# A transformer block on one core: the set-up's loads, modulation, key weights, gates, clears and expert rests in another order

## What is computed

```python
mod = (silu(c) @ wmod).reshape(8, 6, 1, -1)
sa, ca, ga, sb, cb, gb = ...                      # six vectors of 256 for each sequence
ga, gb = sign(g) * max(abs(g), 0.25)
h = layernorm(x) * (1 + ca) + sa
c_q = h @ w_dq.T;  q_c, q_r = c_q @ w_uq.T, c_q @ w_qr.T     # 16 heads of 16 and of 64
c_kv = h @ w_dkv.T;  k_c, v = c_kv @ w_uk.T, c_kv @ w_uv.T
k_r = h @ w_kr.T
q_r, k_r = rope(q_r, k_r)
attn = softmax(causal(([q_c, q_r] @ [k_c, k_r].T) * scale)) @ v
x = x + ga * (attn @ w_out.T)
h = layernorm(x) * (1 + cb) + sb
x = x + gb * experts(h)          # 8 experts of 96, weighted by group from a softmax's top 8 of 32
```

## Time and profile before

| | us |
|---|---|
| median of three runs | 1074.29 |
| lowest and highest run | 1073.05, 1078.35 |
| the profiled execution, its own time | 1071.56 |
| the profiled execution, its span | 1069.9 |

### The profile page before, as it was taken

One profiled execution on the slowest core, in us unless ns is written; L12 is line 12 of the kernel. 1 busy time (PEld: TensorE's weight loads), 2 busy tenths in 40 slices (PEclk: granted clock), 3 DMA queues, 4 the chain that ended last, 5 costly groups with the idle time before them and its releaser, 6 DMA issues.

```text
span 1069.9 us, 23954 instructions
## 1 busy us (share of the span) xinstructions
PE 983.8 (92%) x9847; PEld 724.0 (68%) x9847; DVE 744.9 (70%) x1459; ACT 393.9 (37%) x716; POOL 488.4 (46%) x414
## 2 busy tenths in 40 slices
PE   5899989999899999999899998998989998999887
PEld 4556667766686667866678666865768666776566
DVE  7588586784868768686686848777586876856454
ACT  4234433443333443344332442244323343424322
POOL 1535534645346551654426553374525554266212
PEclk9999989999899998998899998998989999999999
DMA  6421010300102010210102101030011101011000
GB/s 195 119 90 61 2 59 1 100 31 14 48 17 84 31 55 7 69 41 22 60 2 70 61 2 59 2 99 32 16 45 41 59 32 60 1 51 60 2 1 21
DMA packets 37599, 48.73 MB, mean 46 GB/s; under 512 B 9386, under 2 KB 23210, under 8 KB 37490
## 3 DMA queue, kind: packets, MB, share of 16 engines
q1 hardware_dynamic: 37490, 47.20, 13.2%
HBM read 17.80 MB, written 4.21 MB: 21 GB/s over the span
## 4 chain that ended last, share of the span: by engine, by line
PE 73%; DVE 9%; issue 5%; ACT 4%; SPq 3%; POOL 3%; DMA 2%; POOLq 0%; DVEq 0%; ACTq 0%
PE ring L1206 17%; PE ring L1053 11%; PE ring L1054 10%; PE ring L1055 10%; PE av L1222 6%; PE ring L1178 6%; SPq L537 3%; ACT pt L734 3%; DVE prod L916 2%; DVE mcol L940 2%; PE ring L1283 2%; PE ring L1284 2%; PE ring L1285 2%; PE ring L1190 2%; DMA cont<-h_lo 2%
## 5 line engine op out<-in xcount | busy, mean ns | idle before, releaser
L734 ACT ACTIVATE pt<-ring 128x384 f32<-128x384 f32 (+1 forms) x384 | 171.0, 532 | 259.7 <-PE ring L1206 224.6
L940 DVE TENSOR_REDUCE mcol<-ring 128x1 f32<-128x128 f32 (+3 forms) x512 | 212.0, 483 | 44.3 <-PE ring L1183 44.1
L1206 PE MATMUL ring<-rows 32*128 32x512 f32 (+3 forms) x3072 | 189.8, 335 | 9.7 <-issue 2.5
L916 DVE TENSOR_TENSOR prod<-ring,table 128x1024 f32<-128x1024 f32 x128 | 154.2, 1218 | 49.9 <-PE ring L1055 47.9
L1206 PEld LDWEIGHTS ring<-rows 32*128 32x128 f32 x3072 | 137.3, 187 | 67.3 <-issue 35.6
L619 POOL TENSOR_SCALAR_AFFINE_SELECT pt<-pt 128x512 f32<-128x512 f32 x128 | 80.0, 638 | 204.1 <-ACT pt L734 204.0
L592 POOL TENSOR_TENSOR rows<-prod,rows 128x1024 fp32r<-128x1024 f32 x64 | 154.6, 2431 | 7.8 <-ACT rows L713 7.4
L585 POOL TENSOR_TENSOR prod<-prod 128x512 f32<-128x512 f32 x64 | 82.2, 1284 | 158.1 <-DVE prod L916 158.0
L1178 PE MATMUL ring<-rows 32*128 32x512 f32 (+3 forms) x1024 | 78.9, 364 | 20.3 <-ACT pt L734 8.8
L1222 PE MATMUL av<-pt,vals 128*17 128x512 f32 (+3 forms) x1024 | 89.9, 453 | 2.8 <-POOL pt L619 2.8
L1178 PEld LDWEIGHTS ring<-rows 32*128 32x128 f32 x1024 | 44.3, 193 | 63.7 <-issue 37.8
(11 more groups left out here) (188 smaller groups left out, 1858.0 us busy)
## 6 DMA issues: line engine op xcount, KB each, us to landing
cont<-h_hi SPq DMA_DIRECT2D x96, 128.0 KB, 2.0
cont<-h_lo SPq DMA_DIRECT2D x96, 128.0 KB, 2.0
xn<-x_dram SPq DMA_DIRECT2D x8, 512.0 KB, 4.6
xr<-x_dram SPq DMA_DIRECT2D x8, 512.0 KB, 4.2
out_dram<-xr SPq DMA_DIRECT2D x8, 512.0 KB, 3.2
gate_bc<-gates_scratch SPq DMA_DIRECT2D x8, 256.0 KB, 4.8
pt<-wmod_dram SPq DMA_DIRECT2D x1, 1536.0 KB, 6.4
pt<-gup_t_dram SPq DMA_DIRECT2D x16, 96.0 KB, 2.5
```

Of the source, the lines that this page charges most:

```text
L734: sc.activation(pt[:, PT_AT[n] + h * w:PT_AT[n] + (h + 1) * w], ps[:, 0:w], ACT.Exp, scale=SCALE).then_inc(exp_ready.sem, 1)
L916: ve.tensor_tensor(prod[:, s % PROD, :, :], ps[:, :].unsqueeze(1).broadcast_to([P, 2, S]), table[:, :, :], ALU.mult).then_inc(rotated.sem, 1)
L940: last = ve.reduce_max(mcol[:, q, h * HR + ONE_ROW:h * HR + ONE_ROW + 1], ps[:, at:at + (q + 1) * P], AX_X)
L1206: last = pe.matmul(places[h][:, at:at + w], k[head, j * P:(j + 1) * P], q[head, q0:q0 + w], start=p == 0 and at == 0, stop=done, skip_grou ...
```

## The change

The set-up's order and the split of its work are rebuilt. Nothing else is changed but the place of `spread`, which moves from the end of the set-up into the first body.

- Loads: x and the first two of the modulation's six parts go ahead; the other four parts go behind the rotary tables. The register loads of the experts' numbers stand ahead of SP's wait for the modulation, no longer behind it.
- `mod` becomes two steps of 8 products: `mod.0` at the start, `mod.1` and `gates` behind `rope.0011`.
- `split_k` becomes two steps: columns 0 to 255 (subtraction on DVE) and columns 256 to 1,023 (subtraction on GpSimd). ACT rounds both behind the first modulation, no longer ahead of it.
- DVE's clears go to GpSimd (whole tiles), the constants behind the first two rotations.
- The subtraction for the experts' gate and up weights goes from DVE to GpSimd.

```diff
 def setup_steps():
-    out = [("silu",), ("stats1", 0), ("pow1", 0), ("norm1", 0), ("mod",), ("split_d",), ("split_k",), ("turn1", 0, 0), ("turn1", 0, 1),
-           ("gates",), ("modulate1", 0, 0), ("low1", 0, 0), ("modulate1", 0, 1), ("low1", 0, 1), ("fuse", 0), ("split_uv",)]
+    out = [("silu",), ("stats1", 0), ("pow1", 0), ("norm1", 0), ("split_d",), ("mod", 0), ("turn1", 0, 0), ("turn1", 0, 1),
+           ("modulate1", 0, 0), ("low1", 0, 0), ("modulate1", 0, 1), ("low1", 0, 1), ("split_k", 0), ("fuse", 0), ("split_k", 1)]
...
+latent.0 latent_hi.0 latent_lo.0 rope.0000 rotate.0000 rope.0001 rotate.0001 combine.000 consts. split_uv. fuse.1
+kcon.00 kcon_hi.00 kcon_lo.00 move_k.00 rope.0010 rotate.0010 rope.0011 rotate.0011 combine.001 hi.000 mod.1 gates.
...
-            sp.dma_start(wmod_st, wmod.rearrange("(c p) n -> p c n", p=P)).then_inc(ld_mod, 16)
             sp.dma_start(xn[:, :, :], x_rows(0, 0)).then_inc(x_loaded.sem, 16)
+            sp.dma_start(wmod_st[:, :, 0:2 * E], wmod_src[:, :, 0:2 * E]).then_inc(ld_mod, 16)
...
+            sp.dma_start(wmod_st[:, :, 2 * E:6 * E], wmod_src[:, :, 2 * E:6 * E]).then_inc(ld_mod_rest, 16)
...
             sp.wait_ge(ld_idx, 16)
-            sp.wait_ge(mod_read, 1)
+            chosen_at = [sp.value_load(idx_sb[0:1, g:g + 1], min_val=0, max_val=NX - 1) for g in range(G)]
+            sp.wait_ge(mod_read, 2)
             sp.wait_ge(gates_read, 1)
-            chosen_at = [sp.value_load(idx_sb[0:1, g:g + 1], min_val=0, max_val=NX - 1) for g in range(G)]
...
+            pool.wait_ge(mask_made, 1)
+            pool.memset(wuk_l0[:, :].bitcast(F32), 0.0)
+            pool.memset(wuv_l0[:, :].bitcast(F32), 0.0)
+            for part_of in (1, 3):
+                pool.memset(cont[:, :, part_of, :].bitcast(F32), 0.0)
+            pool.memset(spread[:, :].bitcast(F32), 0.0)
+            pool.memset(wT[:, :].bitcast(F32), 0.0).then_inc(pool_setup, 1)
...
+                    if kind == "split_k" and step[1] == 1:
+                        pool.wait_ge(keys_hi_ready, 3)
+                        for k in range(EC):
+                            last = pool.tensor_tensor(keys_to(wk_lo, k, 1), keys_from(k, 1), keys_to(wk_hi, k, 1).bitcast(F32),
+                                                      ALU.subtract)
+                        last.then_inc(keys_lo_rest, 1)
+                    elif kind == "split_ffn":
+                        k = step[1]
+                        pool.wait_ge(ffn_hi_ready, k + 1)
+                        pool.tensor_tensor(gu_lo[:, k, :], gu_st[:, k, :], gu_hi[:, k, :].bitcast(F32), ALU.subtract)\
+                            .then_inc(ffn_split, 1)
...
                         for k in range(EC):
-                            sc.activation(wk_hi[:, k, :].rearrange("p (b h d) -> p b h d", h=HG, d=HALF),
-                                          wk_st[k].rearrange("p (b d h) -> p b h d", h=HG, d=HALF), ACT.Copy)\
-                                .then_inc(keys_hi_ready, 1)
+                            last = sc.activation(keys_to(wk_hi, k, step[1]), keys_from(k, step[1]), ACT.Copy)
+                        last.then_inc(keys_hi_ready, 1)
...
+                    elif kind == "consts":
+
+                        ve.wait_ge(consts_ready, 1)
+                        ve.wait_ge(pool_setup, 5)
...
-                    elif kind == "split_ffn":
-                        k = step[1]
-                        ve.wait_ge(ffn_hi_ready, k + 1)
-                        ve.tensor_tensor(gu_lo[:, k, :], gu_st[:, k, :], gu_hi[:, k, :].bitcast(F32), ALU.subtract)\
-                          .then_inc(ffn_split, 1)
...
+                        pe.wait_ge(ld_mod_rest if step[1] else ld_mod, 16)
...
-                        for which in (0, 1, 3, 4):
+                        for which in (3 * step[1], 3 * step[1] + 1):
...
+                        elif part == "setup" and half == 0:
+                            if g == 0:
+                                pe.wait_ge(keys_split, 2)
+                            else:
+                                pe.wait_ge(keys_lo_rest, 1)
```

More of the change, by code:

```diff
@@ L80 @@
 SETUP_ORDER = """
[L81 removed]
+latent.0 latent_hi.0 latent_lo.0 rope.0000 rotate.0000 rope.0001 rotate.0001 combine.000 consts. split_uv. fuse.1
+kcon.00 kcon_hi.00 kcon_lo.00 move_k.00 rope.0010 rotate.0010 rope.0011 rotate.0011 combine.001 hi.000 mod.1 gates.
+hi.001 lo.000 rope.0100 rotate.0100 fuse.2 fuse.3 rope.0101 rotate.0101 combine.010 lo.001 qcon.00 qcon_hi.00
+qcon_lo.00 move_q.00 values.00 values_out.00 values.01 values_out.01 move_k.01 move_q.01 maxima.000 reduce.000
+rope.0110 rotate.0110 maxima.001 reduce.001 rope.0111 rotate.0111 combine.011 hi.010 maxima.002 reduce.002 lo.010
+split_ffn.0 split_ffn.1 fuse.4 fuse.5 shift.00 shifted.00 hi.011 lo.011 load_late.
 """
@@ L91 @@
[L91 to L105, removed]
@@ L106 @@
-hi.111 store.0 lo.111
+exp.002 move_k.02 value.001 shifted.01 spread. stats1.1 score.010 hi.020 move_q.02 clear.002 hi.021 lo.020 value.002
+rope.0300 exp.010 attn_out.00 lo.021 maxima.020 rotate.0300 rope.0301 reduce.020 pow1.1 score.011 clear.010
+rotate.0301 rope.0310 exp.011 maxima.021 rotate.0310 clear.011 value.010 combine.030 reduce.021 score.012 norm1.1
+rope.0311 exp.012 move_q.03 maxima.022 move_k.03 rotate.0311 clear.012 turn1.10 reduce.022 combine.031 turn1.11
+value.011 modulate1.10 modulate1.11 shift.02 value.012 shifted.02 hi.030 low1.10 score.020 hi.031 attn_out.01
@@ new lines @@
+maxima.030 exp.020 low1.11 wofold.0 score.021 reduce.030 clear.020 maxima.031 exp.021 value.020 reduce.031 clear.021
+lo.030 maxima.032 value.021 reduce.032 score.022 lo.031 shift.03 exp.022 rope.1000 shifted.03 clear.022 score.030
+rotate.1000 value.022 rope.1001 exp.030 attn_out.02 score.031 rotate.1001 clear.030 value.030 exp.031 score.032
+clear.031 combine.100 latent.1 exp.032 qcon.10 hi.100 clear.032 latent_hi.1 value.031 lo.100 qcon_hi.10 latent_lo.1
+value.032 qcon_lo.10 rope.1010 attn_out.03 move_q.10 rope.1011 rotate.1010 kcon.10 mix.00 kcon_hi.10 rotate.1011
@@ new lines @@
+kcon_lo.10 combine.101 mix.01 mixed.00 move_k.10 rope.1100 move_k.11 mixed.01 hi.101 values.10 move_q.11 stats2.0
+values_out.10 maxima.100 rotate.1100 pow2.0 lo.101 norm2.0 reduce.100 turn2.00 turn2.01 rope.1101 modulate2.00
+rope.1110 modulate2.01 low2.00 maxima.101 low2.01 rotate.1101 gate.00 rotate.1110 combine.110 gate.01 tanh.00
+reduce.101 logits.0 tanh.01 hi.110 gated.00 maxima.102 gated.01 logits_copy.0 turn_l.0 reduce.102 up.00 gate.02
+turned_l.0 top.0 up.01 tanh.02 ex.0 top2.0 up.02 gate.03 gated.02 turn_w.0 upped.00 tanh.03 shift.10 upped.01 wT.0
```

96 lines of the change are left out of this document (50 added, 46 removed).

## The result

The changed kernel takes 1086.14 us in the median of five runs (1084.22 to 1086.89), against 1074.29 (1072.97 to 1078.35) for the kernel before: a ratio of 1.0106, 95% interval 1.0084 to 1.0127. Forecast were 1085.0 and slower with 0.82; the measured change is clear of the half per cent that the prediction took as its line. The profiled execution took 1086.89 us, its span 1085.2.

What follows compares the result with a forecast made beforehand. TensorE bounds each sequence, so a set-up delay is handed on; SP's queue delays `maxima.000`. 9.2 (`maxima.000`) + 1.0 (GpSimd's rests) + 1.5 (`spread`) = 11.7 us on 1072.9 gives 1084.6, so 1085; range 1077 to 1091.

Steps and rivals of the forecast that it cites:

- The queue decides M: SP's queue: 16 expert issues ahead of the k and q moves set M at 56, 6.8 us behind q's 49.2.
- M: Start of `maxima.000` on TensorE: 46.80 us before the change, forecast T + 18.0 = 56, so 9.2 us later.
- T: End of DVE's two reading operations of `gates`, which releases SP's expert issues: forecast 37.9 us against 21.9 before.
- The first rival: SP's queue is not the bound: M is q's 49.2, time 1077.8 us; chance 0.12.
- To the latent: Set-up from normalised rows through modulation, ACT's key pieces and `fuse.0`: latent ready at 21.9 us.
- Constants and small splits: DVE work behind the first two rotations, with a rest of `fuse`: 2.80 us as before, ending at 27.2.
- The two ropes: TensorE's ropes behind the rest of `fuse`, ahead of the second modulation half: 2.91 us, ending at 30.1.
- the rival's half clock: TensorE idle about 3.5 us ahead of `kcon.00`, then ropes up to 5.2 instead of 2.9 us: 1088 us; chance 0.10.
- Modulation and gates: TensorE's second half of the modulation, 3.5 us, and `gates`, 3.00 us, behind the ropes, ending at 36.6.
- Behind M: `exp.000` waits for expert rests, now on GpSimd: M + 20.5 instead of M + 19.6, a loss of 1.0 us.
- `spread`, 1.5 us: `spread`, moved on DVE ahead of the next statistics, delays the maxima TensorE waits for: 1.5 us (0 to 2.4).
- The head start: First rotation starts 8.0 us earlier; as a rival, M follows it and the kernel takes 1064.9 us; chance 0.04.

Runs made afterwards that it cites:

- the hole filled: The changed kernel plus 40 unread products of 128 x 512 on TensorE in the idle stretch ahead of `maxima.000`: 1083.48 us.
- the first version built on the result: The changed kernel with one load per expert, k and q moves ahead of those loads, `mod.1` and `gates` behind `qcon.00`, latent and constants earlier: 1070.58 us.
- the one before the last: The first version built on the result, reordered: small splits ahead of the latent, `fuse.1` to `fuse.3` ahead of their ropes, `mod.1` and `gates` behind `maxima.000`: 1067.3 us.
- the last: The one before the last with `mod.1`, `gates` and expert loads back behind `rope.0101`, three late `gates` operations behind `lo.011`: 1065.2 us.
- the one with TensorE busy early: The first version built on the result plus 16 unread TensorE products ahead of the first modulation and 12 behind the first transposes: 1079.5 us.

## Why the prediction was right, step by step

**The queue decides M: shown.** M was T + 17.8 (forecast T + 18.0), and the 16 issues took 12.09 us. Releasing SP earlier, issuing half of the loads later, or halving the number of issues each brought M to 52.5 to 54.9, and late gates alone made 9.6 us in the kernel before. The first rival ("the queue is not the bound") falls. Its M of 49.2 was 3.6 us too early, as was my q: q was ready at 49.52 and not at 45.9, so with 3.3 of transfer M would have been 52.8, and it was 52.51 with half of the issues behind. So of M's 12.4 us the queue made 6.4 (forecast 6.8), and the other 6.0 are the later q. The Trainium skill's "DMA: Bandwidth & Descriptors", section "Issuing engines are not separate DMA queues", calls the time to initiate a DMA usually small beside the DMA itself. For one load the rows agree: an expert load of 96 KB took 0.76 us of the queue and landed 2.5 us (median) behind its issue. For a series they don't: the transfers overlapped and the issues added up, to 12.09 us, for which the moves had to wait.

**T was mis-sized: 41.4 instead of 37.9, just past its upper bound of 41.** The input's part was right: power at 8.34 (8.3), rows normalised at 10.78 (10.7). Then:
- *To the latent*, 24.46 instead of 21.9. `fuse.0` waited for the query weights until 15.37, and its four products took 4.08 us at half speed; my sum had them hidden, but ACT waited 2.63 us for them ahead of its next piece.
- *Constants and small splits*, 4.6 us behind the rotations instead of 2.80: beside GpSimd's work DVE's operations took longer (1.69 and 1.17 above, against 0.75 and 0.20 in the kernel before).
- *The two ropes*, 3.84 us instead of 2.91: the rival's half clock did come behind the hole of 3.43 us (granted clock 0.66 in 31.54 to 36.40), but cost 0.9 us and not 2.3.
- *In between*, 1.0 that I had not counted: the first rotation waited 0.49 us for a rope at half speed, and `kcon.00`, also at half speed, held the ropes back by 0.5.
- *Modulation and gates*, 3.7 us instead of 6.5: my prices stood on rows at half speed. This gave 2.8 us back.

**Behind M: right in size, by another cause.** I had `score.000` unchanged and 1.0 us lost to GpSimd's rests. Measured: 21.66 us from M to 80.84, against 20.22 before, so 1.4, and `exp.000` at M + 21.0 (forecast 20.5) with GpSimd as the releaser. But `score.000` alone was 1.3 us late, at a clock of 0.79 (0.88 in the kernel before). With the hole filled it followed in 13.22 us, `exp.000` came at M + 19.6, still behind GpSimd, and TensorE went on at M + 20.2 as before the change. The long idle stretch cost more here than its length; GpSimd's rests stand just behind.

**`spread`, 1.5 us: the step that failed.** Put back, it gave nothing that the times show, and in its new place TensorE never waited for DVE in that stretch (80.84 to 103.45). The 1.3 us lost there go with a granted clock of 0.92, where before had 1.00 (the same 254 products kept TensorE busy for 21.99 us instead of 20.52); with one load for each expert, and `spread` in its new place, the same stretch took 21.52 us at 1.00. So it is the clock, and a row with DVE as releaser (0.16 us of wait at 92.23) was no evidence for a price of 1.5. That the term's 1.5 and the clock's 1.3 are alike is luck.

**The sum** of 11.7 us is 3.6 short of the 15.3 between the two profiled spans, and nearly all of that is T (M 12.4 later instead of 9.2; behind M 0.4 more; 1.3 of clock where I had 1.5 for `spread`). That it meets the 11.85 between the medians is luck: the two executions that were profiled lie 3.5 us further apart than the medians, about as much as T was short.

**The head start** (rotations from 24.95 instead of 29.94) was real and lost, as its rival said. With the moves ahead of the expert issues alone it still didn't get through (M 46.45); with TensorE's order changed too it did in part: M 39.26 and 42.04, 1067.3 and 1065.2 us.

**What stays open.** The time from `score.000` to the end of the span was 1009 us in the kernel before. It is 7 us shorter in the first version built on the result and in the one before the last, 4 in the last, and not shorter in the one with TensorE busy early. The order of the sequences is the same in all. Windows over that whole time, of the kernel before and of the version before the last:

```profile
60.73:1069.00 1008.27, 940.17 (x9641) 695.03 (x9641) 703.66 (x1376) 371.56 (x678) 466.02 (x381) 0.96 0.12 40
```

```profile
63.67:1066.28 1002.61, 935.48 (x9641) 692.92 (x9641) 695.47 (x1375) 369.15 (x676) 469.93 (x383) 0.96 0.12 40
```

The same 9,641 products kept TensorE busy for 4.7 us less, while its idle time differs by 1.0: most of the difference lies in the pace of the products, thus in the granted clock, which the column rounds to 0.96 in both. So part of the gain of these versions is not the set-up's own time. What in the set-up decides how the clock falls in the sequences, no run tells.

## What to carry to other kernels

Before a step is moved later, look at what is queued behind its release on each issuing engine: 16 cheap-looking loads that lay in a hole became a 12 us barrier in front of six moves. The number of issues is a cost of its own, here by the load and not by the byte; put urgent transfers ahead of long series, and merge the series. A price from the trace holds at the clock and beside the neighbours with which it was measured: ask what both are in the new place.

## What the runs showed of the hardware

**An operation of DVE takes longer beside GpSimd's.** The same subtractions on DVE's timeline, first in the first version built on the result, with the row of GpSimd's key rests that run beside them (its first rotation sum follows at 30.01), then in the version before the last, with GpSimd idle.

```profile
28.37 1.75 DVE L854 TENSOR_TENSOR gw_lo<-pt,gw_hi 128x64 fp32r<-128x64 f32 x1 [0.33 <-ACT wuk_hh L698]
30.05 1.51 DVE L855 TENSOR_TENSOR wuv_l<-gate_bc,wuv_hh 64x256 fp32r<-64x256 f32 x1
...
27.73 2.31 POOL L609 TENSOR_TENSOR wk_lo<-room,wk_hi 128x768 fp32r<-128x768 f32 x1
```

```profile
19.66 0.23 DVE L854 TENSOR_TENSOR gw_lo<-pt,gw_hi 128x64 fp32r<-128x64 f32 x1 [0.34 <-ACT wuk_hh L698]
19.80 0.41 DVE L855 TENSOR_TENSOR wuv_l<-gate_bc,wuv_hh 64x256 fp32r<-64x256 f32 x1
```

The 128 x 64 subtraction took 1.75 against 0.23 us, the 64 x 256 one 1.51 against 0.41: work handed to GpSimd was not free for DVE, even where nobody waited for its result. This agrees with the Trainium skill, "Trainium Architecture — The Big Picture", section "What this means for kernel authors": DVE and GpSimd share a pair of ports, which one of them holds alone.

**The clock column is blind at the start.** In 7.30 to 10.85 it reads 1.00, but 16 modulation products took 3.55 us there and 1.85 at 36.40, and in the version with products ahead of them 1.85 at 8.23. They ran at half the pace, as at the lower of the clock's two levels, and the column did not show it. The spacing of equal products tells more than the column there.
